# A message-passing layer in one fused kernel: source rows spread by transfers, row tiles every nine chunks, six more picks

## The chip, the cores and the metric

The kernel runs on one core of one Trainium2 chip. The time is device time in microseconds, from start to end of one execution, and lower is better. A core has five engines that run their own instruction streams and meet at semaphores: TensorE (PE, with its weight loads PEld), VectorE (DVE), ScalarE (ACT), GpSimd (POOL) and SyncE (SP). Transfers are sent from the queues of SyncE and ScalarE, and, where they gather rows by an index, from GpSimd.

## What is computed

One layer of a graph network over 6250 nodes and 200000 edges, with 64 features on each, then a residual sum and a layer norm. The edges are sorted by `dst`; `src` is random.

```python
features = H[id_Xe[0]]                                   # H = x, id_Xe = (src, dst)
M_in = jnp.concatenate([features, Xe], axis=1)           # Xe = edge_attr
Y = jax.nn.relu(M_in @ M_W.T + M_b)
Z = jax.ops.segment_sum(Y, id_Xe[1], num_segments=H.shape[0])
H_next = jax.nn.relu(jnp.concatenate([H, Z], axis=1) @ U_W.T + U_b)
out = _layernorm(x + H_next)
```

## The kernel before

The product of the message matrix with the node part is made once for each node, not for each edge: `Y = x @ Wn.T + M_b`, kept in SBUF and stored to DRAM as `Y_rows`. Then the edges go by in 195 chunks of 1024 (8 tiles of 128), and a rest of 320 edges, which the code calls chunk 195 (`NC`). For each chunk the row of Y at each edge's source must be added to the product of its edge features. There are three ways to get those rows for a tile:

- **gathered** (line 399): GpSimd sends one indirect transfer for each tile, which reads 128 rows of `Y_rows` by index (of `x` itself in the first 5 chunks).
- **picked** (lines 705, 731, 741, 949): the sources of the tile are spread over all partitions, ScalarE subtracts the partition's own number (`match`, line 522), VectorE compares the result with the start of each of the 49 blocks of nodes (`onehot_src`, one instruction of 128x6272 elements), and TensorE multiplies the result with Y, 49 products in bf16 on three parts of Y side by side. VectorE sums the three parts. Tile 7 of every chunk from 5 on is picked, and tile 6 too in the chunks that `picked_tiles` names: 249 picks.
- **row by row** (line 368, `load_rows` of SyncE): for tile 6 of the chunks in `row_chunks` SyncE loads node numbers into its registers and sends one transfer of 256 B for each row. The 128 rows of a tile are spread over the steps of several chunks before it (`row_steps`). ScalarE copies the tile into its place (`copy_rows`, line 535).

The rest of a chunk c: SyncE loads the edges (lines 331 and 332, three buffers; it waits until the transposes of chunk c-3 are done), TensorE turns them (line 900), ScalarE copies them (line 508), TensorE multiplies them with the edge weights (`add_edges`, line 918), VectorE adds the rows of Y (`add_rows`, line 725), which waits for that chunk's gathers, ScalarE rectifies (line 528), TensorE sums the messages by destination with a one-hot window of 72 nodes (line 956), and VectorE adds the window to `XZ` (line 749).

Each engine's order is written out by hand. TensorE in round c: edges of c, windows of c-1, transposes of c+1, `spread_src(c + 2)` (line 936), picks of c+1. `spread_src` is a product of one column of the identity with the sources, kept as floats in `src_ones`, and puts a row of 128 or 256 sources onto all partitions of `p_bc`. ScalarE in round c: copy of the turned edges of c+1, match of c+2, rectification of c, copy of a row tile of c+1. VectorE in round c: sums of the picks of c, window comparison of c, window of c-1, `add_rows(c)`, then `copy_match` and comparison for c+2. GpSimd gathers up to six chunks ahead (`G = 6`, it waits for `s_rows_added`), and afterwards adds and multiplies by the means and deviations of the layer norm. After the last chunk come the update product (lines 1002 and 1013) and the layer norm in groups of 8 blocks.

Of the kernel before, what the change touches and what calls it, by code (L numbers as in the profile page):

```python
# [6 lines left out]
def gnn_residual_layernorm_kernel(  # L7
# [13 lines left out]
    i32 = mybir.dt.int32  # L21
# [5 lines left out]
    P = 128  # L27
# [37 lines left out]
    def picked_tiles(c):  # L65
        if not X <= c < NC:
            return []
        return [TILES - 2, TILES - 1] if c % 3 == 0 and c % 48 else [TILES - 1]

    ROWS_TILE = TILES - 2
    ROWS_EVERY = 12
    ROWS_AT_ONCE = 12
    row_chunks = [c for c in range(2 * ROWS_EVERY + 1, NC, ROWS_EVERY) if ROWS_TILE not in picked_tiles(c)]
    row_steps = {row_chunks[t] - s: (t, P - s * ROWS_AT_ONCE - ROWS_AT_ONCE)
                 for t in range(len(row_chunks)) for s in range(-(-P // ROWS_AT_ONCE))}
# [32 lines left out]
                edge_values[T1:NE].rearrange("(p j) -> p j", p=TP))  # L110

    edge_tail = (edge_attr[T0:T1, :].rearrange("(p j) d -> p (j d)", p=P), edge_attr[T1:NE, :])
    dst_tail_row = dst[T0:NE].rearrange("(c n) -> c n", c=1)
    x_blocks = x[0:NFULL * W, :].rearrange("(b p) d -> p b d", p=W)
    out_blocks = out[0:NFULL * W, :].rearrange("(b p) d -> p b d", p=W)
# [2 lines left out]
    with ctx:  # L118
        def sb(name, shape, dt=fp32):
            return ctx.enter_context(nc.sbuf_tensor(name, shape, dt))  # L120
# [7 lines left out]
        def sem(name):  # L128
# [14 lines left out]
        messages = [sb(f"messages{u}", [P, TILES * D]) for u in range(SLOTS)]  # L143
        onehot = [sb(f"onehot{u}", [P, TILES, WIN]) for u in range(SLOTS)]
        onehot_src = [sb(f"onehot_src{u}", [P, NW, P], bf16) for u in range(SLOTS)]
        match = [sb(f"match{u}", [P, 2 * P], i16) for u in range(2)]

        XZ = sb("XZ", [P, NW * W + W])
# [21 lines left out]
        u_bias = sb("u_bias", [D, 1])  # L170

        src_rows = [onehot_src[1][:, 8 * h:8 * h + 16, :].rearrange("p b e -> p (b e)").bitcast(i32)
                    for h in (0, 2)]
        dst_rows = [XZ[:, h * CHUNK:(h + 1) * CHUNK].bitcast(i32) for h in range(2)]
        src_float = [onehot_src[0][:, 16 * h:16 * h + 16, :].rearrange("p b e -> p (b e)").bitcast(fp32)
                     for h in range(2)]
        src_ones = [sb(f"src_ones{h}", [P, CHUNK - RUN]) for h in range(2)]
        dst_float = [onehot_src[2][:, 16 * h:16 * h + 16, :].rearrange("p b e -> p (b e)").bitcast(fp32)  # L180
                     for h in range(2)]
        dst_tail = sb("dst_tail", [1, TAIL], i32)
# [48 lines left out]
        s_dst_tail_loaded = sem("s_dst_tail_loaded")  # L231
        s_src_float = sem("s_src_float")
        s_dst_float = sem("s_dst_float")
        s_src_ones = sem("s_src_ones")
        s_index_T = sem("s_index_T")
        s_index_even = sem("s_index_even")
        s_index_odd = sem("s_index_odd")
# [29 lines left out]
        s_chunk_added = sem("s_chunk_added")  # L267
        s_window = sem("s_window")
        s_window_added = sem("s_window_added")
        s_src_spread = sem("s_src_spread")  # L270
        s_match = sem("s_match")
        s_match_copied = sem("s_match_copied")
        s_onehot_src = sem("s_onehot_src")
# [113 lines left out]
        @block.gpsimd  # L387
        def _(pool):
            nc.gpsimd.memset(ident[:, :], 0.0).then_inc(s_ident, 1)
            pool.wait_ge(s_ident, 1)  # L390
            nc.gpsimd.affine_select(out=ident[:, :], in_=ident[:, :], compare_op=ALU.not_equal, fill=1.0,
                                    base=0, pattern=[[-1, P]], channel_multiplier=1).then_inc(s_ident, 1)
            nc.gpsimd.iota(count[:, :], pattern=[[1, WIN]], base=0, channel_multiplier=0)
            nc.gpsimd.iota(window_start_i[:, :], pattern=[[WIN, NWIN]], base=0, channel_multiplier=0)
            nc.gpsimd.iota(block_start_i[:, :], pattern=[[W, NW]], base=0, channel_multiplier=0)
            nc.gpsimd.iota(node_i[:, :], pattern=[[1, 1]], base=0, channel_multiplier=1).then_inc(s_iota, 1)

            def gather(c, j, index, table, parts=P):
                nc.gpsimd.indirect_dma_start(  # L399
                    out=gathered[c % G][0:parts, j * D:(j + 1) * D], out_offset=None, in_=table,  # L400
                    in_offset=bass.IndirectOffsetOnAxis(ap=index, axis=0),
                ).then_inc(s_gathered[c % G], 16)

            pool.wait_ge(s_src_first_loaded, 16)
            for c in range(X):
                for j in gathered_tiles(c):
                    gather(c, j, src_first[:, c, j:j + 1], x[:, :])

            pool.wait_ge(s_Y_stored, 16 * stores)
            pool.wait_ge(s_index_even, 2)  # L410
            pool.wait_ge(s_index_odd, 2)
            for c in range(X, NC):
                if c >= G:

                    pool.wait_ge(s_rows_added, c - G + 1)
                for j in gathered_tiles(c):
                    gather(c, j, src_all[:, c, j:j + 1], Y_rows)
            pool.wait_ge(s_src_last_loaded, 2 * 16)
            pool.wait_ge(s_rows_added, NC - G + 1)
            for j in gathered_tiles(NC):  # L420
                parts = TP if j == TT - 1 else P
                gather(NC, j, src_last[0:parts, j:j + 1], Y_rows, parts)

            def apply_to_rows(g, values, op, done):
                b0, b1 = groups[g]
                nc.gpsimd.tensor_tensor(h[:, b0:b1, :], h[:, b0:b1, :],  # L426
                                        values[:, b0:b1].unsqueeze(2).to_broadcast([P, b1 - b0, D]),
                                        op).then_inc(done, 1)

            for g in range(len(groups) + LAG + 1):  # L430
                if g < len(groups):
                    pool.wait_ge(s_mean, g + 1)
                    apply_to_rows(g, mean, ALU.add, s_centered)
                if g > LAG:
                    pool.wait_ge(s_scale, g - LAG)
                    apply_to_rows(g - LAG - 1, std, ALU.mult, s_normed)

        @block.scalar
        def _(act):
# [10 lines left out]
            act.dma_start(dst_tail[:, :], dst_tail_row).then_inc(s_dst_tail_loaded, 16)  # L450
            act.dma_start(dst_first[:, :, :], first_chunks(dst)).then_inc(s_dst_first_loaded, 16)

            act.wait_ge(s_eps, 1)
            nc.scalar.activation(std[:, 0:1], eps_col[:, 0:1], ACT.Sqrt)

# [19 lines left out]
                rows_to_float(h0, dst_rows, dst_float, s_dst_rows_loaded, s_dst_float)  # L475
            copy_even_index(4, dst_all)
            copy_even_index(6, dst_all)
            for h0, (b0, n) in enumerate(halves):
                nc.scalar.copy(src_ones[h0][0:n, :], src_rows[h0][0:n, RUN:CHUNK]).then_inc(s_src_ones, 1)

            def copy_block_start(b0, b1):
                nc.scalar.copy(block_start[:, b0:b1, :], block_start_i[:, b0:b1].unsqueeze(2)  # L482
                               .to_broadcast([P, b1 - b0, P])).then_inc(s_block_start, 1)
# [31 lines left out]
            def match_src(c):  # L515

                q, n = c - X, len(picks_of[c]) * P
                act.wait_ge(s_src_spread, q + 1)
                if q >= 2:

                    act.wait_ge(s_match_copied, q - 1)
                nc.scalar.activation(match[q % 2][:, 0:n], p_bc[:, 0:n], ACT.Identity,  # L522
                                     bias=minus_node[:, 0:1]).then_inc(s_match, 1)

            def rectify(c):
# [15 lines left out]
            copy_edges_T(0)  # L541
            copy_x_rows_T(0)
            for c in range(NC + 1):
                if c < NC:
                    copy_edges_T(c + 1)
                if c + 1 < X:
                    copy_x_rows_T(c + 1)
                if picks_of[c + 2]:
                    match_src(c + 2)
                rectify(c)  # L550
                if c + 1 in row_chunks:
                    copy_rows(c + 1)
                if c < 2:
                    copy_middle(c)
                    copy_block_start((0, X_FIRST)[c], (X_FIRST, NW)[c])
                elif X < c <= X + 2:
                    two = c - X - 1
                    nc.scalar.copy(x_rows_of[:, :, two, :], pairs_T[two * D:(two + 1) * D, :, :])
                elif c == X + 3:
                    nc.scalar.copy(XZ[0:D, NFULL * W:NW * W],  # L560
                                   x_pairs_T[0:D, NFULL // 2 * W:(NFULL // 2 + 1) * W]).then_inc(s_XZ, 1)
# [260 lines left out]
        def _(pe):  # L822
# [101 lines left out]
                                                w_gathered[:, :], start=False, stop=(q == PAIRS - 1))  # L924
                last.then_inc(s_summed, 1)

            def spread_src(c):

                q, j = c - X, picked_tiles(c)[0]
                h0, n = (0, P) if c < P else (1, NB)  # L930
                if q == 0:
                    pe.wait_ge(s_src_ones, 2)
                if q >= 1:

                    pe.wait_ge(s_match, q)
                nc.tensor.matmul(p_bc[:, 0:(TILES - j) * P],  # L936
                                 ident[0:n, c - h0 * P:c - h0 * P + 1].to_broadcast([n, P]),
                                 src_ones[h0][0:n, j * P - RUN:CHUNK - RUN],
                                 start=True, stop=True).then_inc(s_src_spread, 1)

            def pick(k):
                if k == 0:
                    pe.wait_ge(s_Y_low, 2)
# [27 lines left out]
            def chunks(windows):  # L971
                transpose_edges(0)
                transpose_x_rows(0)
                for c in range(NC + 1):
                    add_edges(c)
                    if c > 0:
                        windows(c - 1)
                    if c < NC:
                        transpose_edges(c + 1)
                    if c + 1 < X:  # L980
                        transpose_x_rows(c + 1)
                    if picks_of[c + 2]:
                        spread_src(c + 2)
                    for k in picks_of[c + 1]:
                        pick(k)
                windows(NC)
# [61 lines left out]
```

## Time and profile before

| | |
|---|---|
| median of three runs | 1671.68 us (1670.69 to 1673.19) |
| the profiled execution | 1672.69 us, its span 1670.8 us |
| TensorE busy | 1630.3 us, 98% |
| VectorE busy | 1327.9 us, 79% |
| GpSimd busy | 1242.5 us, 74% |
| ScalarE busy | 322.4 us, 19% |
| granted TensorE clock, mean | 0.994 of full speed |

The profile is of one execution. An engine's busy time leaves out its gaps and the instructions that only issue a transfer, so 74% does not say yet how much room an engine has: whether an engine waits for another is told by its waits, and by the order of its instructions in time. Lines are those of the kernel file.

### The profile page before, as it was taken

What the parts mean: (1) busy time and instruction counts of PE and PEld (TensorE: products, weight loads), DVE (VectorE), ACT (ScalarE), POOL (GpSimd) and SP (SyncE); (2) the same over time, 40 slices, a digit from 0 to 9 for tenths busy, and PEclk for the clock granted to TensorE, in tenths of its full rate; (3) what the DMA queues carried; (4) which work ended last, traced back from release to release, by engine and by line L of the source; (5) the groups of instructions that cost most, each with busy time, mean ns of one, the idle gap of its engine ahead of it and who ended that gap; (6) DMA issues with size and microseconds to landing.
All of it is one profiled execution on the core that took longest, in us unless ns stands there. A gap on an engine that the chain in (4) does not pass through costs nothing.

```text
span 1670.8 us, 48392 instructions
## 1 busy us (share of the span) xinstructions
PE 1630.3 (98%) x18304; PEld 1564.1 (94%) x18304; DVE 1327.9 (79%) x1364; ACT 322.4 (19%) x662; POOL 1242.5 (74%) x1323
## 2 busy tenths in 40 slices
PE   5899999999999999999999999999999999999995
PEld 5899999999999999999999999999999999999992
DVE  5787887887888888788788788788778878878873
ACT  4431111111111111111111111111111111111113
POOL 6777777777777777777777777777777777777773
PEclk9999999999999999999999999999999999999997
DMA  7222222222222222222222222222222222222221
GB/s 167 64 65 58 56 66 60 55 66 59 60 60 60 60 59 60 60 60 60 66 60 60 60 60 60 59 61 60 60 59 60 65 55 60 63 57 59 66 43 41
DMA packets 147453, 104.09 MB, mean 62 GB/s; under 512 B 100874, under 2 KB 125418, under 8 KB 147216
## 3 DMA queue, kind: packets, MB, share of 16 engines
q0 software_dynamic: 41568, 42.63, 13.2%
q1 hardware_dynamic: 104530, 56.69, 13.2%
q8 instruction: 148, 2.42, 0.6%
q10 hardware_dynamic: 1118, 1.62, 0.4%
q14 instruction: 89, 0.73, 0.2%
HBM read 97.62 MB, written 3.20 MB: 60 GB/s over the span
## 4 chain that ended last, share of the span: by engine, by line
PE 96%; DVE 1%; ACT 1%; issue 0%; DMA 0%; POOL 0%; DVEq 0%; SPq 0%; POOLq 0%; ACTq 0%
PE p_pick L949 60%; PE p_messages L956 13%; PE p_messages L918 11%; PE p_edges_T L900 7%; PE p_bc L936 3%; PE p_messages L1002 1%; DMA u_stage<-in_L_gnn_U_W_dram 0%; ACT block_start L482 0%; DVE XZ L684 0%; POOL Y L426 0%; PE p_messages L857 0%; PE p_edges_T L868 0%; DVE onehot_src L741 0%; PE p_pick L832 0%; ACT Y_parts L493 0%
## 5 line engine op out<-in xcount | busy, mean ns | idle before, releaser
L399 POOL DMA_INDIRECT gathered<-Y_rows,src_all x1256 | 1185.3, 944 | 383.0 <-issue 379.6
L949 PE MATMUL p_pick<-Y_parts,onehot_src 128*128 128x192 bf16 x12201 | 1037.8, 246 | 0.4 <-DVE onehot_src L741 0.4
L949 PEld LDWEIGHTS p_pick<-Y_parts,onehot_src 128*128 128x128 bf16 x12201 | 1012.6, 98 | 10.6 <-issue 0.7
L741 DVE TENSOR_TENSOR onehot_src<-p_dve,block_start 128x6272 bf16<-128x6272 int16 x249 | 847.1, 3421 | 6.5
L508 ACT COPY edges_T<-p_edges_T 128x512 f32<-128x512 f32 x196 | 114.5, 584 | 1174.3 <-PE p_edges_T L900 1174.3
L956 PE MATMUL p_messages<-onehot,messages 128*64 128x72 f32 x3126 | 237.5, 229 | 2.0 <-ACT messages L528 2.0
L956 PEld LDWEIGHTS p_messages<-onehot,messages 128*64 128x64 f32 x3126 | 208.5, 137 | 25.6 <-ACT messages L528 2.5
L918 PE MATMUL p_messages<-w_edges,edges_T 128*128 128x128 f32 x1564 | 213.0, 279 | 4.9 <-ACT edges_T L508 4.8
L918 PEld LDWEIGHTS p_messages<-w_edges,edges_T 128*128 128x128 f32 x1564 | 190.7, 192 | 6.2 <-ACT edges_T L508 3.4
L705 DVE TENSOR_REDUCE gathered<-p_pick 128x64 f32<-128x192 f32 x249 | 86.9, 349 | 92.6 <-PE p_pick L949 92.6
L696 DVE SCALAR_TENSOR_TENSOR onehot<-p_dve,base,dst_all 128x576 f32<-128x576 f32 x195 | 157.4, 807 | 0.0
L749 DVE TENSOR_TENSOR XZ<-XZ,p_messages 64x72 f32 x196 | 45.7, 233 | 135.6 <-PE p_messages L956 133.6
L528 ACT ACTIVATE messages<-p_messages 128x512 f32<-128x512 f32 x196 | 117.0, 597 | 130.9 <-DVE p_messages L725 128.0
L725 DVE TENSOR_TENSOR p_messages<-p_messages,gathered 128x512 f32<-128x512 f32 x191 | 133.3, 698 | 6.5 <-issue 0.6
L900 PE MATMUL p_edges_T<-ident,edges 128*128 128x128 f32 x782 | 128.4, 287 | 2.9 <-issue 2.9
L900 PEld LDWEIGHTS p_edges_T<-ident,edges 128*128 128x128 f32 x782 | 82.1, 141 | 18.1 <-issue 3.0
L731 DVE TENSOR_SCALAR p_dve<-match 128x64 int32<-128x64 int32 x190 | 46.6, 245 | 57.8 <-ACT match L522 57.8
L936 PE MATMUL p_bc<-src_ones,ident 128*128 128x128 f32 (+1 forms) x380 | 85.9, 308 | 0.0
L522 ACT ACTIVATE match<-p_bc,minus_node 128x128 int16<-128x128 f32 x190 | 77.1, 406 | 0.0
L936 PEld LDWEIGHTS p_bc<-src_ones,ident 128*128 128x128 f32 (+1 forms) x380 | 57.4, 191 | 0.0
L399 POOL DMA_INDIRECT gathered<-in_x_dram,src_first x40 | 40.5, 1012 | 15.3 <-issue 11.9
L426 POOL TENSOR_TENSOR Y<-Y,mean 128x512 f32<-128x512 f32 (+1 forms) x7 | 6.5, 934 | 21.7 <-DVE mean L800 21.7
(101 smaller groups left out, 203.0 us busy)
## 6 DMA issues: line engine op xcount, KB each, us to landing
edges<-in_edge_attr_dram SPq DMA_DIRECT2D x190, 192.0 KB
row_tile<-Y_rows SPq DMA_DIRECT2D x1920, 0.2 KB
gathered<-Y_rows,src_all POOLq DMA_INDIRECT x1256
edges<-in_edge_attr_dram SPq DMA_DIRECT2D x191, 64.0 KB
Y_rows<-Y SPq DMA_DIRECT2D x6, 256.0 KB
out_dram<-Y SPq DMA_DIRECT2D x6, 256.0 KB
edges<-in_edge_attr_dram SPq DMA_DIRECT2D x5, 256.0 KB
xb<-in_x_dram SPq DMA_DIRECT2D x1, 768.0 KB
```

Source lines behind the costliest of these rows:

```text
L399: nc.gpsimd.indirect_dma_start(out=gathered[c % G][0:parts, j * D:(j + 1) * D], out_offset=None, in_=table, in_offset=bass.IndirectOffsetO ...
L508: nc.scalar.copy(edges_T[c % SLOTS][:, 0:pairs * P], p_edges_T[:, 0:pairs * P]).then_inc(s_edges_T_copied, 1)
L528: nc.scalar.activation(messages[c % SLOTS][:, 0:pairs * P], p_messages[c % SLOTS][:, 0:pairs * P], ACT.Relu).then_inc(s_messages, 1)
L696: nc.vector.scalar_tensor_tensor(out=onehot[c % SLOTS][:, 0:tiles, :], in0=count_b[:, 0:tiles, :], scalar=start, in1=nodes.unsqueeze(2).to ...
L705: nc.vector.tensor_reduce(gathered[c % G][:, j * D:(j + 1) * D], p_pick[k % 2][:, 0:3 * D].rearrange("p (t d) -> p d t", d=D), AX.X, ALU.a ...
L725: nc.vector.tensor_tensor(sums, sums, gathered[c % G][:, 0:cols], ALU.add).then_inc(s_rows_added, 1)
L741: nc.vector.tensor_tensor(onehot_src[k % SLOTS][:, :, :], sources.unsqueeze(1).to_broadcast([P, NW, P]), block_start[:, :, :], ALU.is_equa ...
L900: last = nc.tensor.transpose(p_edges_T[:, q * P:(q + 1) * P], edges[u][:, q * P:(q + 1) * P], ident[:, :])
L918: last = nc.tensor.matmul(p_messages[u][:, q * P:(q + 1) * P], edges_T[u][:, q * P:(q + 1) * P], w_edges[:, :], start=(q == 0), stop=(c >= ...
L936: nc.tensor.matmul(p_bc[:, 0:(TILES - j) * P], ident[0:n, c - h0 * P:c - h0 * P + 1].to_broadcast([n, P]), src_ones[h0][0:n, j * P - RUN:C ...
L949: last = nc.tensor.matmul(p_pick[k % 2][:, 0:3 * D], onehot_src[k % SLOTS][:, b, :], Y_parts[:, b, :], start=(b == 0), stop=(b == NW - 1))
L956: last = nc.tensor.matmul(p_windows[u], messages[u][:, j * D:(j + 1) * D], onehot[u][:, j, :], start=(j == 0), stop=(j == tiles - 1))
```

## The change

- `picked_tiles`: tile 6 is picked in every chunk whose number divides by 3, and in those with c % 72 == 4 (76 and 148). 255 picks instead of 249.
- A row tile in every ninth chunk instead of every twelfth, 20 instead of 15, with 16 rows in each step instead of 12.
- The spread of the sources leaves TensorE. ScalarE issues, four chunks ahead, a transfer that reads 128 or 256 sources of the chunk from DRAM and writes them to all 128 partitions of `src_spread` (three buffers, a semaphore for each). The match reads that buffer. In ScalarE's order the match and this transfer stand ahead of the copy of the turned edges. Three of the transfers are issued at the very start.
- GpSimd has a drain between its last gather and the update.

```diff
-        return [TILES - 2, TILES - 1] if c % 3 == 0 and c % 48 else [TILES - 1]
+        return [TILES - 2, TILES - 1] if c % 3 == 0 or c % 72 == 4 else [TILES - 1]
-    ROWS_EVERY = 12
-    ROWS_AT_ONCE = 12
+    ROWS_EVERY = 9
+    ROWS_AT_ONCE = 16
...
+        src_spread = [sb(f"src_spread{u}", [P, 2 * P], i32) for u in range(SLOTS)]
...
+            pool.drain()
+
             def apply_to_rows(g, values, op, done):
...
+            def spread_src(c):
+
+                q, j = c - X, picked_tiles(c)[0]
+                if q >= SLOTS:
+
+                    act.wait_ge(s_match, q - SLOTS + 1)
+                act.dma_start(src_spread[q % SLOTS][:, 0:(TILES - j) * P],
+                              src_chunks[c][:, j * P:CHUNK].to_broadcast([P, (TILES - j) * P])
+                              ).then_inc(s_src_spread[q % SLOTS], 16)
+
+            for c in range(X, X + SLOTS):
+                spread_src(c)
...
-            for h0, (b0, n) in enumerate(halves):
-                nc.scalar.copy(src_ones[h0][0:n, :], src_rows[h0][0:n, RUN:CHUNK]).then_inc(s_src_ones, 1)
...
-                act.wait_ge(s_src_spread, q + 1)
+                act.wait_ge(s_src_spread[q % SLOTS], 16 * (q // SLOTS + 1))
...
-                nc.scalar.activation(match[q % 2][:, 0:n], p_bc[:, 0:n], ACT.Identity,
+                nc.scalar.activation(match[q % 2][:, 0:n], src_spread[q % SLOTS][:, 0:n], ACT.Identity,
...
             for c in range(NC + 1):
+                if picks_of[c + 2]:
+                    match_src(c + 2)
+                if X + SLOTS <= c + 4 < NC:
+                    spread_src(c + 4)
                 if c < NC:
                     copy_edges_T(c + 1)
                 if c + 1 < X:
                     copy_x_rows_T(c + 1)
-                if picks_of[c + 2]:
-                    match_src(c + 2)
...
-            def spread_src(c):
...
-                nc.tensor.matmul(p_bc[:, 0:(TILES - j) * P],
-                                 ident[0:n, c - h0 * P:c - h0 * P + 1].to_broadcast([n, P]),
-                                 src_ones[h0][0:n, j * P - RUN:CHUNK - RUN],
-                                 start=True, stop=True).then_inc(s_src_spread, 1)
...
-                    if picks_of[c + 2]:
-                        spread_src(c + 2)
```

## Rows read from the trace of the kernel before

**Rows 1.** The page: the chain that ended last, shares of the span by line

```profile
PE p_pick L949 60%; PE p_messages L956 13%; PE p_messages L918 11%; PE p_edges_T L900 7%; PE p_bc L936 3%; PE p_messages L1002 1%; DMA u_stage<-in_L_gnn_U_W_dram 0%; ACT block_start L482 0%; DVE XZ L684 0%; POOL Y L426 0%; PE p_messages L857 0%; PE p_edges_T L868 0%; DVE onehot_src L741 0%; PE p_pick L832 0%; ACT Y_parts L493 0%
```

**Rows 2.** The chain in order of time: start us, us, what

```profile
107.84 0.22 PE p_bc L936 x2
108.07 4.04 PE p_pick L949 x49
...
114.76 0.43 PE p_bc L936 x2
```

**Rows 3.** GpSimd's waits (us, times, longest); line 399's duration ns min/median/max, first and last start

```profile
POOL gathered L399 <- issue: 392.5, 1287, 0.3
POOL Y L426 <- DVE mean L800: 21.7, 6, 15.4
POOL gathered L399 <- DVE p_messages L725: 3.0, 10, 0.3
...
L399 POOL DMA_INDIRECT gathered<-Y_rows,src_all x1256: 940/944/961, 58.0 to 1625.1; - x180
```

**Rows 4.** Timeline at the loop's end: start us, us, engine, line, op [idle before]

```profile
1625.07 0.94 POOL L399 DMA_INDIRECT gathered<-Y_rows,src_all  x1 [0.30 <-issue]
...
1628.81 0.91 POOL L399 DMA_INDIRECT gathered<-Y_rows,src_last  x1 [0.30 <-issue]
...
1629.54 0.70 DVE L725 TENSOR_TENSOR p_messages<-p_messages,gathered 128x512 f32<-128x512 f32 x1
...
1632.56 0.37 DVE L725 TENSOR_TENSOR p_messages<-p_messages,gathered 128x192 f32<-128x192 f32 x1
```

**Rows 5.** Stretch of 200 us: busy PE, PEld, DVE, ACT, POOL, clock, DMA share

```profile
200.00:400.00 200.00, 200.00 (x2291) 193.92 (x2289) 162.96 (x160) 34.17 (x75) 151.07 (x161) 1.00 0.27 60
```

**Rows 6.** Timeline: the last gather from x and who reads it

```profile
56.80 0.94 POOL L399 DMA_INDIRECT gathered<-in_x_dram,src_first  x1 [0.30 <-issue]
...
59.55 0.60 PE L907 MATMUL p_pick<-ident,gathered 128*128 128x128 f32 x4
```

**Rows 7.** Timeline of SyncE's queue

```profile
135.28 4.81 SPq L368 DMA_DIRECT2D row_tile<-Y_rows  x12
...
703.70 0.37 SPq L331 DMA_DIRECT2D edges<-in_edge_attr_dram  x1
704.11 1.36 SPq L332 DMA_DIRECT2D edges<-in_edge_attr_dram  x1
706.64 4.85 SPq L368 DMA_DIRECT2D row_tile<-Y_rows  x12
711.54 0.36 SPq L331 DMA_DIRECT2D edges<-in_edge_attr_dram  x1
...
718.12 0.44 SPq L332 DMA_DIRECT2D edges<-in_edge_attr_dram  x1
719.49 3.20 SPq L368 DMA_DIRECT2D row_tile<-Y_rows  x8
...
1597.84 4.84 SPq L368 DMA_DIRECT2D row_tile<-Y_rows  x12
```

**Rows 8.** SyncE's waits: us in total, times, longest

```profile
SPq L331 <- PE p_edges_T L900: 400.0, 97, 10.1
```

**Rows 9.** Timeline of ScalarE in the loop

```profile
729.93 0.26 ACT L535 COPY gathered<-row_tile 128x64 f32<-128x64 f32 x1
...
817.55 0.58 ACT L508 COPY edges_T<-p_edges_T 128x512 f32<-128x512 f32 x1 [5.58 <-PE p_edges_T L900]
```

**Rows 10.** Timeline of the first issues, and the landing of the bias broadcast

```profile
0.76 0.45 SPq L310 DMA_DIRECT2D src_first<-in_src_dram  x1
...
0.76 1.06 ACTq L443 DMA_DIRECT2D onehot_src<-in_src_dram  x2
...
14.98 0.77 SPq L319 DMA_DIRECT2D m_bias<-in_L_gnn_M_b_dram  x1
...
m_bias<-in_L_gnn_M_b_dram SPq DMA_DIRECT2D x1, 32.0 KB, 4.0
```

More of the change, by code:

```diff
@@ L112, in gnn_residual_layernorm_kernel @@
     edge_tail = (edge_attr[T0:T1, :].rearrange("(p j) d -> p (j d)", p=P), edge_attr[T1:NE, :])
+    src_chunks = src[0:NC * CHUNK].rearrange("(c a n) -> c a n", a=1, n=CHUNK)
     dst_tail_row = dst[T0:NE].rearrange("(c n) -> c n", c=1)
@@ L178, in gnn_residual_layernorm_kernel @@
                      for h in range(2)]
-        src_ones = [sb(f"src_ones{h}", [P, CHUNK - RUN]) for h in range(2)]
         dst_float = [onehot_src[2][:, 16 * h:16 * h + 16, :].rearrange("p b e -> p (b e)").bitcast(fp32)
@@ L233, in gnn_residual_layernorm_kernel @@
         s_dst_float = sem("s_dst_float")
-        s_src_ones = sem("s_src_ones")
         s_index_T = sem("s_index_T")
@@ L269, in gnn_residual_layernorm_kernel @@
         s_window_added = sem("s_window_added")
-        s_src_spread = sem("s_src_spread")
+        s_src_spread = [sem(f"s_src_spread{u}") for u in range(SLOTS)]
         s_match = sem("s_match")
@@ L925, in add_edges @@
                 last.then_inc(s_summed, 1)
-            def spread_src(c):
[L929 to L935, printed above, removed]
-                nc.tensor.matmul(p_bc[:, 0:(TILES - j) * P],
-                                 ident[0:n, c - h0 * P:c - h0 * P + 1].to_broadcast([n, P]),
-                                 src_ones[h0][0:n, j * P - RUN:CHUNK - RUN],
-                                 start=True, stop=True).then_inc(s_src_spread, 1)
             def pick(k):
```

## Prediction

> **What bounds the kernel now.** I read the page first: the chain that ended last runs over TensorE's lines, 60 + 13 + 11 + 7 + 3% of the span, and the 3% is the line this change deletes [rows 1]. That suggests TensorE alone sets the pace. The chain in order of time gives the prices of its pieces: a pick is 4.04 us; from its end (112.11 us) to the next spread at 114.76 us a chunk takes 2.65 us for its products, windows and transposes; the spread itself is 0.22 us for one tile of sources and 0.43 us for two [rows 2].
>
> Then I asked who waits on the other engines, since a second engine may stand just behind. GpSimd spends nearly nothing on waiting: 3.0 us for VectorE, and 392.5 us of "issue", which is 1287 gaps of 0.3 us, one before each gather [rows 3]. So it issues its gathers back to back from 5.4 to 1629.7 us, 1299 of them (40 + 1256 + 3) with hardly a pause. The last four start from 1625.07 to 1628.81, three periods of 1.247 us [rows 4]. The durations run from 940 to 961 ns over all 1256 [rows 3], so the period is a fixed price. The last gather ends at 1629.7 us and VectorE adds the last rows at 1632.56 us [rows 4]: GpSimd arrives only 2.8 us before it is needed. The kernel has two bounds that finish together.
>
> SyncE is the third. In its queue a step of one chunk is two edge loads, a stretch that loads the node numbers into registers, and twelve row transfers; the step from 703.70 to 711.49 us leaves 0.05 us before the next edge load starts at 711.54 [rows 7]. Its total spare time is 400.0 us of waiting for TensorE's transposes [rows 8].
>
> **Part 1, the spread leaves TensorE.** 190 spreads go, 131 of one tile and 59 of two: 131 x 0.22 + 59 x 0.43 = 54.2 us off TensorE's path [rows 2]. Six picks come (249 to 255: chunks 48, 96, 144 and 192 by the first clause, 76 and 148 by the second), 6 x 4.04 = 24.2 us. TensorE's own sum is 30.0 us shorter.
>
> **Part 2, GpSimd.** Five more row tiles (15 to 20) and six more picks take 11 gathers away: 11 x 1.247 = 13.7 us, so its last gather ends at 1629.7 - 13.7 = 1616.0 us. This is the smaller of the two savings, so GpSimd becomes the bound and some 16 us of TensorE's gain turn into waits of VectorE's addition for gathers. Per nine chunks GpSimd issues 3 x (7 + 7 + 6) - 1 = 59 gathers, 73.6 us, while TensorE needs 9 x 2.65 + 12 x 4.04 = 72.3 us [rows 2]. VectorE is busy 163 of 200 us in the loop [rows 5]; it has room to catch up behind a late gather, so such a delay isn't cumulative.
>
> Behind the last gather comes its landing time L. The trace has no landing for gathers. The nearest row: the last gather from x (L399, gathered<-in_x_dram) ends at 57.74 us and TensorE reads its tile at 59.55 us, straight after its previous work [rows 6], so L is at most 1.8 us there, and at least 0. I take 1.8. From the last addition at 1632.56 us to the end of the span 38.2 us pass and stay as they are. New span: 1616.0 + 1.8 + 38.2 = 1656.0 us. The addition of chunk 194 can't be in the way: it needs 3.0 us to the next addition (1629.54 to 1632.56), and the three last gathers take 3.7 us.
>
> What a page says of L: the Trainium skill, "DMA: Bandwidth & Descriptors", section "Anatomy of one DMA — SWDGE (gpsimd) path", gives such a transfer a fixed cost of about 2.0 us from issue to completion. The trace agrees as far as it goes (at most 0.94 + 1.8 us from start to use). Counted so, as an estimate, the last rows would be there at 1615.1 + 2.0 us and the span 0.7 us shorter.
>
> **Part 3, SyncE.** Rows go from 1920 to 2560, in steps of 16. Over the 143 full steps of twelve, from 135.28 to 1597.84 us [rows 7], the edge loads, register loads and rows take 7.02 us in the mean (I averaged the timeline; single ones run 6.8 to 7.4). Four rows more cost (4.93 - 3.23) = 1.70 us by the difference between the mean twelve and the mean of the 15 first steps of eight, or 4 x 0.41 by the mean per row; the register stretch ahead of the rows grows from 0.93 us (eight rows, 718.56 to 719.49) to 1.17 (twelve, 705.47 to 706.64), so another 0.2 for four [rows 7]. A step of 16 is 8.9 us, with the gap behind it 8.94. Eight steps and a chunk without rows (0.98 us) are 72.5 us per nine chunks, against GpSimd's 73.6. It is hidden with only 1.1 us to spare in each tile. Within a tile the steps run behind the transposes by up to 8 x 8.9 - 55 - 8.9 = 7 us (55 us is what TensorE needs for seven chunks, two of them with two picks: 7 x 2.65 + 9 x 4.04). The rows of one tile end at 711.49 us, 7.8 us after the trigger of their step (703.70), and ScalarE copies them at 729.93 us, 26 us after it [rows 7, 9]. Now 7 + 8.9 = 16 us plus a landing are set against those 26: still in time. The edge loads have three chunks (some 24 us) of lead: hidden.
>
> **Part 4, ScalarE.** Each chunk gains one transfer issue. No row shows one in the loop; bounds from the start: 0.53 us for a plain load on this queue, 0.77 us for a broadcast to 128 partitions on SyncE's [rows 10]. I take 0.6. After its rectification ScalarE sits idle 5.58 us until the next transposes [rows 9]; the match and the issue fit there, as the transfer was sent two chunks ahead (the bias broadcast took 4.0 us to land [rows 10], two chunks are 16 us). Behind the match wait the copy of the transposed edges and the rectification; both are released later anyway. If that cover were gone, 190 x 0.6 us would be 114 us, but ScalarE is busy 34 of 200 us [rows 5]. At the start three issues stand ahead of ScalarE's first conversion: TensorE begins 1.6 to 2.3 us later. GpSimd's first 40 gathers don't depend on it, so it costs nothing now. VectorE loses its 57.8 us of waits for the match, which was no bound.
>
> **Part 5, the drain.** It stands after the last gather, where GpSimd waits 15.4 us for the first mean [rows 3]: between 0 and that, taken as 0.
>
> **Sum.** Span 1656.0 us. The span of before is 1670.8, its execution 1672.69, the median of the three runs 1671.68: 0.9 above the span. Forecast 1656.9 us.
>
> **Rivals.**
> *A, GpSimd bound, as above:* 1655.1 (L = 0) to 1659 us (L = 4), 0.62.
>
> *B, SyncE becomes the bound.* Mechanism: the row tile's last step comes too late, ScalarE waits at the copy of the rows, and copies of transposed edges queue behind that. For: 1.1 us of spare per tile, some second edge loads of 1.36 us instead of 0.44 [rows 7], and a queue of ScalarE that now sends a row to each of 128 partitions in every chunk beside it. Against: the first issues of both queues ran side by side at 0.45 and 0.53 us each, less than the later 0.77 alone [rows 10], and the DMA engines are busy 27% [rows 5]. The Trainium skill says in the same page, section "Issuing engines are not separate DMA queues", that transfers started by any engine end up on the same 16 DMA engines and interleave; it gives no price for that. Price: the first step starts near 97 us; twenty periods P = 8s + 1, the five chunks behind the last row tile (38 us) and the tail (38) give a span of 172 + 20P. It passes 1656 at s = 9.15 us and 1671 at s = 9.24. With 0.5 us of contention in each step (s = 9.45) the span is 1704. Slower by over 0.2%: 0.17; between, 1660 to 1672: 0.05.
>
> *C, small stalls:* VectorE's comparison starts only after a late addition, two-pick chunks then start picking late, and the end finds TensorE behind: 3 to 10 us. For: the three engines are within 2% of each other; against: GpSimd never waits for them, having six buffers. 1659 to 1667 us, 0.11.
>
> *D, TensorE was the only bound:* 1671.7 - 30.0 + 1 = 1643 us, would need gathers faster than the 940 ns minimum: 0.02.
>
> *E, nothing moves:* something keeps the end where it is, 1670 to 1673: 0.03.
>
> **Chances and range.** What a measurement of this kernel tells from no change is 0.2%, 3.3 us. Faster: A, C, D and most of the middle of B, 0.78; same 0.05; slower 0.17. The range reaches from A's lower bound over C and B's middle: 1654.5 to 1669 us.
>
> **What would show it.** GpSimd: 1248 gathers in the loop and after it, period 1.247 us, the last ending near 1616 us. VectorE's addition (line 725) with some 15 us of new idle before it, and TensorE with as much. SyncE's steps near 8.9 us with 20 to 90 us of waiting for transposes left. ScalarE's copy of rows with no wait before it. I am wrong if SyncE's steps pass 9.15 us, if gathers take longer than 944 ns, or if GpSimd waits for buffers.

## The result, and the profile after

The changed kernel takes 1654.38 us in the median of four runs (1653.16 to 1655.23), the kernel before beside it 1672.09 us. The ratio is 0.9894, with a 95% interval of 0.9880 to 0.9908. Faster was forecast, and it is; but the time was forecast as 1656.9 us with a range from 1654.5 to 1669 us, and lies 2.5 us below the forecast and just under the range.

The page of the changed kernel: span and busy times, then the chain that ended last by engine and line, and three groups (line, engine, operation, count; busy, mean ns of one; idle time before and what ended it).

```profile
span 1651.4 us, 50341 instructions
PE 1602.5 (97%) x18218; PEld 1542.1 (93%) x18218; DVE 1337.4 (81%) x1376; ACT 338.0 (20%) x665; POOL 1231.4 (75%) x1312
...
POOL 69%; issue 23%; PE 5%; DVE 1%; ACT 1%; ACTq 0%; DMA 0%; POOLq 0%; DVEq 0%
POOL gathered L398 69%; PE p_pick L949 2%; PE p_messages L1000 1%; PE p_messages L956 1%; PE p_messages L932 0%; DVE XZ L698 0%; POOL Y L428 0%; PE p_edges_T L914 0%; PE p_edges_T L882 0%; PE p_messages L871 0%; PE p_messages L937 0%; PE p_pick L846 0%; DVE most L646 0%; ACT block_start L494 0%; DVE least L645 0%
...
L398 POOL DMA_INDIRECT gathered<-Y_rows,src_all x1245 | 1175.2, 944 | 379.6 <-issue 379.3
...
L739 DVE TENSOR_TENSOR p_messages<-p_messages,gathered 128x512 f32<-128x512 f32 x191 | 133.3, 698 | 93.0 <-DMA gathered<-Y_rows,src_all 73.7
```

TensorE is still busy 97%, and yet the chain has changed its engine. Before, it ran over TensorE's lines from start to end [rows 1]; now 69% of the span is the gathers themselves and 23% the gaps before them. The mean gather is as long as before, 944 ns [rows 3]. New is that VectorE's addition waits 73.7 us for gathers, 50 times; before, it had no such wait. Busy shares would have told none of this.

The waits of the changed kernel (engine line <- who ended the wait: us in total, times, longest).

```profile
ACT messages L540 <- DVE p_messages L739: 296.5, 121, 5.9
DVE p_messages L739 <- DMA gathered<-Y_rows,src_all: 73.7, 50, 4.5
...
PE p_messages L956 <- ACT messages L540: 7.7, 4, 4.6
...
PE p_pick L949 <- DVE onehot_src L755: 5.8, 9, 1.3
...
SPq L330 <- PE p_edges_T L914: 66.0, 21, 9.9
```

VectorE's 73.7 us of waiting are mostly absorbed by queued work: TensorE itself waits 13.5 us in these two lines. SyncE's waiting for transposes has gone from 400.0 us [rows 8] to 66.0.

The end of the loop in the timeline of the changed kernel (start us, us, engine, line).

```profile
1612.76 0.70 DVE L739 TENSOR_TENSOR p_messages<-p_messages,gathered 128x512 f32<-128x512 f32 x1 [4.46 <-DMA gathered<-Y_rows,src_all]
...
1614.04 0.90 POOL L398 DMA_INDIRECT gathered<-Y_rows,src_last  x1 [0.30 <-issue]
1614.14 2.18 PE L956 MATMUL p_messages<-onehot,messages 128*64 128x72 f32 x16 [4.62 <-ACT messages L540]
1616.47 0.23 DVE L763 TENSOR_TENSOR XZ<-XZ,p_messages 64x72 f32 x1 [2.54 <-PE p_messages L956]
1616.73 0.37 DVE L739 TENSOR_TENSOR p_messages<-p_messages,gathered 128x192 f32<-128x192 f32 x1
```

The last gather ends at 1614.94 us, against 1629.72 before [rows 4], and the last addition starts 1.79 us behind it.

**Where 19.4 us of span went** (1670.8 to 1651.4): the last gather ends 14.8 us earlier (13.7 were forecast), the stretch from it to the last addition is 1.05 us shorter (2.84 to 1.79), and the stretch from there to the end is 3.6 us shorter (38.2 to 34.7), where none was forecast. The two profiled executions lie apart by more than the medians, 19.5 us against 17.7: the one of before was 0.6 us slower than the median of the four runs of that kernel, the one of the changed kernel was the fastest of its four, 1.2 us below their median.

Most of what made the last part shorter stands in the instructions of line 118 (before) and 119 (after), the end of the program. First the kernel before, then the changed one (duration ns min/median/max, first and last start us), each with GpSimd's last multiplication (start us, us) from the timeline.

```profile
L118 POOLq DRAIN  x1: 8518/8518/8518, 1662.0 to 1662.0; - x1
L118 SPq COMPARE_BRANCH  x1: 38/38/38, 1667.8 to 1667.8; - x1
L118 SPq DRAIN  x1: 7/7/7, 1668.0 to 1668.0; - x1
...
1660.87 3.29 POOL L426 TENSOR_TENSOR Y<-Y,std 128x512 f32<-128x512 f32 x4
```

```profile
L119 POOLq DRAIN  x1: 2206/2206/2206, 1645.2 to 1645.2; - x1
...
L119 SPq DRAIN  x1: 7/7/7, 1651.1 to 1651.1; - x1
...
1644.00 3.29 POOL L428 TENSOR_TENSOR Y<-Y,std 128x512 f32<-128x512 f32 x4
```

Before, SyncE had seen its last store land and reached its own drain at 1668.0 us, but GpSimd's closing drain ran until 1670.5. After, GpSimd's is over at 1647.4 and SyncE is the last. That is 2.5 us, as much as the miss. The experiments below test it. A closing drain's record starts while GpSimd's last multiplications still run: before, it ends 6.4 us behind them, after, 0.1 us. So of the 8.5 us some 2 are ordinary work, and so are the 2.2 us of the changed kernel.

### The profile page after: what moved, and what is told of

Its sections match the earlier page's. It is cut to its first block, busy times and chain, and to the rows that moved or that the text cites. A ratio compares the mean times of both kernels' runs of the same rounds, so it can differ in the third digit from the quotient of the medians.

```text
span 1651.4 us, 50341 instructions
## 1 busy us (share of the span) xinstructions
PE 1602.5 (97%) x18218; PEld 1542.1 (93%) x18218; DVE 1337.4 (81%) x1376; ACT 338.0 (20%) x665; POOL 1231.4 (75%) x1312
## 4 chain that ended last, share of the span: by engine, by line
POOL 69%; issue 23%; PE 5%; DVE 1%; ACT 1%; ACTq 0%; DMA 0%; POOLq 0%; DVEq 0%
POOL gathered L398 69%; PE p_pick L949 2%; PE p_messages L1000 1%; PE p_messages L956 1%; PE p_messages L932 0%; DVE XZ L698 0%; POOL Y L428 0%; PE p_edges_T L914 0%; PE p_edges_T L882 0%; PE p_messages L871 0%; PE p_messages L937 0%; PE p_pick L846 0%; DVE most L646 0%; ACT block_start L494 0%; DVE least L645 0%
## 5 line engine op out<-in xcount | busy, mean ns | idle before, releaser
L949 PE MATMUL p_pick<-Y_parts,onehot_src 128*128 128x192 bf16 x12495 | 1061.9, 246 | 6.8 <-DVE onehot_src L755 5.8
L949 PEld LDWEIGHTS p_pick<-Y_parts,onehot_src 128*128 128x128 bf16 x12495 | 1035.7, 98 | 11.5 <-issue 8.2
L755 DVE TENSOR_TENSOR onehot_src<-p_dve,block_start 128x6272 bf16<-128x6272 int16 x255 | 867.0, 3421 | 6.5
L739 DVE TENSOR_TENSOR p_messages<-p_messages,gathered 128x512 f32<-128x512 f32 x191 | 133.3, 698 | 93.0 <-DMA gathered<-Y_rows,src_all 73.7
L534 ACT ACTIVATE match<-src_spread,minus_node 128x128 int16<-128x128 int32 x190 | 81.8, 431 | 0.0
L1000 PE MATMUL p_messages<-XZ,w_update 128*64 128x512 f32 (+1 forms) x26 | 14.8, 662 | 2.5 <-issue 2.5
L846 PE MATMUL p_pick<-ident,onehot_src 128*128 128x128 f32 (+1 forms) x32 | 7.0, 386 | 6.6 <-DVE dst_all L640 3.6
```

The source lines that it names most:

```text
L534: nc.scalar.activation(match[q % 2][:, 0:n], src_spread[q % SLOTS][:, 0:n], ACT.Identity, bias=minus_node[:, 0:1]).then_inc(s_match, 1)
L739: nc.vector.tensor_tensor(sums, sums, gathered[c % G][:, 0:cols], ALU.add).then_inc(s_rows_added, 1)
L755: nc.vector.tensor_tensor(onehot_src[k % SLOTS][:, :, :], sources.unsqueeze(1).to_broadcast([P, NW, P]), block_start[:, :, :], ALU.is_equa ...
L949: last = nc.tensor.matmul(p_pick[k % 2][:, 0:3 * D], onehot_src[k % SLOTS][:, b, :], Y_parts[:, b, :], start=(b == 0), stop=(b == NW - 1))
```

## The experiments

My theory: the end of the kernel is the latest of three queues that hardly wait for each other, GpSimd's gathers, TensorE's products and SyncE's row steps; the change takes TensorE from the first to the second place. The rivals: TensorE alone; SyncE already; and, for the missing 2.5 us, chance in the profile or the drain.

**One part alone: the spread.** `picked_tiles`, `ROWS_EVERY` and `ROWS_AT_ONCE` are those of before, all else is the changed kernel.

```diff
-        return [TILES - 2, TILES - 1] if c % 3 == 0 or c % 72 == 4 else [TILES - 1]
+        return [TILES - 2, TILES - 1] if c % 3 == 0 and c % 48 else [TILES - 1]
-    ROWS_EVERY = 9
-    ROWS_AT_ONCE = 16
+    ROWS_EVERY = 12
+    ROWS_AT_ONCE = 12
```

> The spread of the sources is sent by ScalarE as in the change; picks (249), row tiles (15) and rows per step (12) are those of before, and so are the 1256 gathers. My theory, GpSimd's chain of gathers sets the end: TensorE has 54 us less to do and the time hardly moves. GpSimd's last gather should end at 1628.6 us (the start of the Y gathers 1.3 us earlier, as after the change), and 1.8 us plus the tail of 34.7 to 38.2 us behind it give a span of 1665 to 1668.6 us. Rival, TensorE alone is the bound: 54 us less, a span near 1617 us. Also: if the issues on ScalarE are what brought the Y gathers forward, they start at 56.7 us here; if not, at 58.0.

Measured: 1667.79 us (1666.73 to 1670.63), a ratio of 0.9974 (0.9962 to 0.9985), span 1668.7 us. TensorE has 54 us less to do and the kernel gains 4.3 us, of which the drain, which this kernel also has and which alone gives 2.8 us (below), can explain a good half. The Y gathers start at 57.1 us, between the two values that I had set against each other, so that side question stays open here. The last gather ends at 1631.7 us, 3 us later than forecast, since a gather takes 947 ns in the median in this execution instead of 944; this execution is the slowest of seven, 2.8 us above their median. The waits say where the 54 us went.

```profile
ACT messages L540 <- DVE p_messages L739: 480.2, 158, 5.9
...
DVE p_messages L739 <- DMA gathered<-Y_rows,src_all: 157.4, 87, 5.2
...
PE p_pick L949 <- DVE onehot_src L755: 36.6, 43, 1.3
```

TensorE now stands still before 43 picks, because the comparisons for them start behind additions that wait for gathers. TensorE as the only bound falls.

**The other part alone: the counts.** The kernel before with the three settings of the change, the spread still on TensorE.

```diff
-        return [TILES - 2, TILES - 1] if c % 3 == 0 and c % 48 else [TILES - 1]
+        return [TILES - 2, TILES - 1] if c % 3 == 0 or c % 72 == 4 else [TILES - 1]
-    ROWS_EVERY = 12
-    ROWS_AT_ONCE = 12
+    ROWS_EVERY = 9
+    ROWS_AT_ONCE = 16
```

> 255 picks, 20 row tiles and 16 rows per step, with the spread left on TensorE as before. TensorE's sum grows by 6 picks (24.2 us) and six wider spreads (1.3 us) while GpSimd saves 11 gathers (13.7 us). My theory, the later of the two ends counts: TensorE, span 1670.8 + 25.5 = 1696 us. Rival, gathers alone decide: 1657 us. SyncE, at 9.0 us for each step, has room again since the chunks are longer.

Measured: 1699.69 us (1698.63 to 1700.2), ratio 1.016 (1.0143 to 1.0177), span 1698.3 us. The chain is TensorE's again (96%) and GpSimd waits for means instead of the other way round:

```profile
PE 96%; DVE 1%; ACT 1%; issue 0%; DMA 0%; POOL 0%; DVEq 0%; SPq 0%; POOLq 0%; ACTq 0%
...
POOL Y L426 <- DVE mean L800: 55.1, 6, 48.8
...
SPq L118 <- PEq L118: 4.7, 1, 4.7
```

The forecast of 1696 is short by 2.3 us; in this run SyncE waits 4.7 us at the end of the program for GpSimd's closing drain, which took 10478 ns, where the kernel before waits 2.7 us. So the two halves are worth -4 us (with the drain) and +28 us alone, and -18 us together. They don't add up: each moves a different queue, and only the later one counts.

**How far GpSimd's bound reaches: 8 and 24 gathers less.** The changed kernel without the gather of tile 0 in every 24th, or every 8th, chunk. It leaves out rows that the result needs and keeps the other instructions, so it shows a time and computes other messages. Shown for every 24th chunk, which is 8 gathers less:

```diff
-                if j not in picked_tiles(c) and not (c in row_chunks and j == ROWS_TILE)]
+                if j not in picked_tiles(c) and not (c in row_chunks and j == ROWS_TILE) and not (j == 0 and c % 24 == 2 and c > 2)]
```

> The kernel after the change with 8 gathers left out (tile 0 of every 24th chunk keeps what its buffer held, so those messages use other rows). My theory: GpSimd ends 8 x 1.248 = 10.0 us earlier and the span follows it, 1651.4 - 10.0 = 1641.4 us, since TensorE's own end lies near 1638 to 1641 us of span (1670.8 - 30.0, and up to 3 us of shorter tail). Rival, SyncE or TensorE already sets the pace after the change: the span stays within 3 us of 1651.

> The kernel after the change with 24 gathers left out (tile 0 of every 8th chunk keeps what its buffer held). GpSimd alone would end 30 us earlier, at a span of 1621 us. My theory: TensorE takes over, so the span stops at its floor of 1638 to 1641 us. If SyncE's row steps are the next bound (20 periods of 73.0 us from 97 us on, and 75 us behind them) that alone would be 1631 us, below TensorE's. Rival, no other bound within 30 us: 1621 us.

Measured: 1643.65 us (span 1641.7) without 8, and 1639.93 us (span 1638.8) without 24; ratios to before 0.9828 (0.9812 to 0.9845) and 0.9802 (0.9786 to 0.9819). The first 8 gathers give 9.7 us of span, 1.2 us each, a gather's full period. The next 16 give 2.9 us instead of 20. (The medians say 10.7 and 3.7 us.) The chains of the two kernels, 8 gathers less first:

```profile
PE 46%; POOL 37%; issue 13%; DVE 2%; ACT 1%; ACTq 0%; DMA 0%; POOLq 0%; DVEq 0%
```

```profile
PE 96%; DVE 1%; ACT 1%; issue 0%; ACTq 0%; POOL 0%; DVEq 0%; POOLq 0%
...
POOL Y L428 <- DVE mean L814: 36.3, 6, 30.0
```

TensorE's floor is a span of 1638.8 us, 12.6 below the changed kernel. GpSimd is the bound there, and TensorE is next.

**SyncE's turn: one more transfer in each row step.** The changed kernel, with a 17th row per step, into a tile that nobody reads.

```diff
+        row_extra = sb("row_extra", [P, D])
...
+        s_extra = sem("s_extra")
...
+                sp.dma_start(row_extra[r0 // ROWS_AT_ONCE:r0 // ROWS_AT_ONCE + 1, :], Y_rows[0:1, :]).then_inc(s_extra, 16)
                 for r, end in zip(range(r0, r1), ends):
...
+            sp.wait_ge(s_extra, 16 * len(row_steps))
```

> The kernel after the change, and in each of the 160 row steps SyncE sends one more row, into a tile that nobody reads. A step grows from 8.96 to 9.37 us. Theory of the third bound: nine chunks then need 8 x 9.42 + 0.98 = 76.3 us of SyncE, more than GpSimd's 73.6; the last row lands near 97 + 20 x 76.3 = 1623 us instead of 1571, and with the 72 us behind it the span is 1693 to 1698 us, while GpSimd begins to wait for free buffers. Rival, SyncE still has its 66 us of waits to spend: 160 x 0.41 = 66 us are absorbed, and the span stays at 1651 to 1655 us.

Measured: 1669.17 us (1663.92 to 1670.29), ratio 0.9978 (0.9965 to 0.9992), span of the profiled execution 1662.1 us. Neither number came true as written. The mechanism came true in part: SyncE has 21% of the chain, and the copy of rows and the transposes now wait for its transfers. But GpSimd does not begin to wait for buffers, as I had expected: its gathers run on undisturbed (5 waits of at most 0.3 us for VectorE, the last gather starts at 1614.4 us).

```profile
PE 38%; POOL 23%; SPq 21%; issue 14%; DVE 2%; DMA 2%; ACT 1%; ACTq 0%; DVEq 0%; POOLq 0%
...
ACT gathered L551 <- DMA row_tile<-Y_rows: 31.6, 11, 4.4
...
PE p_edges_T L918 <- DMA edges<-in_edge_attr_dram: 15.5, 12, 3.2
```

The size was off because I priced the extra row at 0.41 us. That is a row whose address comes from a register. This one has a fixed address:

```profile
815.32 0.27 SPq L368 DMA_DIRECT2D row_extra<-Y_rows  x1
815.78 6.41 SPq L370 DMA_DIRECT2D row_tile<-Y_rows  x16
822.24 0.36 SPq L332 DMA_DIRECT2D edges<-in_edge_attr_dram  x1
```

From edge load to edge load the step takes 9.19 us in the mean of 155 steps, against 9.02 in the changed kernel (156 steps). The prediction's formula, 172 + 20 x (8 x 9.19 + 0.98), gives a span of 1662.0 us, and 1662.1 was measured in the profiled execution. That it fits to the tenth is luck: this is the fastest of five executions, and three of the others have spans of 1667.4 to 1668.5 us. So 0.17 us more in a step of 9.02 moves the end from GpSimd to SyncE and costs over 10 us of span, 14.8 us in the median.

**The drain, taken away.** One line less in the changed kernel.

```diff
-            pool.drain()
```

> The changed kernel without GpSimd's drain. It stands where GpSimd waits 13 us for the first mean, so I expect no difference: within 1 us of the changed kernel, 1653.5 to 1655.5 us. If the drain cost its wait for transfers at the end, or shortened the tail, this would differ by 1 us or more.

Measured: 1659.77 us (1659.07 to 1660.16), ratio 0.9926 (0.991 to 0.9943), against 0.9894 (0.9880 to 0.9908) with it: 5.4 us slower. I had expected no difference, and that was wrong. The end of the program in this kernel:

```profile
L119 POOLq DRAIN  x1: 10483/10483/10483, 1647.6 to 1647.6; - x1
L119 SPq COMPARE_BRANCH  x1: 38/38/38, 1653.4 to 1653.4; - x1
...
SPq L119 <- PEq L119: 4.7, 1, 4.7
```

The closing drain takes 10.5 us instead of 2.2 and ends 4.5 us after everything else. The remaining 0.9 us of the medians lies within their intervals. The two profiled executions lie 7.0 us apart: besides the 4.5, the gathers start 1.1 us later here (57.8 against 56.7 us, long before any drain) and end 1.3 us later, and the first mean comes 1.1 us later behind the last addition.

**The drain, added alone.** The kernel before with nothing but that line.

```diff
+
+            pool.drain()
```

> The kernel before with nothing but GpSimd's drain behind its last gather. In the kernel before the drain at the end of the program takes 8518 ns, and ends at 1670.5 us, 2.5 us after SyncE is done at 1668.0; with the earlier drain that closing one took 2206 ns in four runs. My theory: the early drain does this work under GpSimd's wait for the first mean, the closing drain shrinks to 2.2 us, and the time falls by 2.5 us, to a ratio of 0.9985. Rival, the early drain only moves the same work or costs its own: no change or slower by up to 1 us.

Measured: 1669.56 us (1668.35 to 1671.38, 11 runs), ratio 0.9986 (0.9977 to 0.9995), the expected one. In its trace the closing drain is short. The early one's record starts while gathers still run, and reaches to 1635.4 us: 6.4 us behind the end of the last gather (1629.0) and well ahead of the first mean (1643.0), for which GpSimd waits anyway:

```profile
L424 POOLq DRAIN  x1: 21282/21282/21282, 1614.1 to 1614.1; - x1
```

```profile
L118 POOLq DRAIN  x1: 2207/2207/2207, 1660.0 to 1660.0; - x1
```

Both directions agree, so the drain's gain is shown; its size is less sharp, as the interval of this run alone reaches from 0.8 to 3.8 us. The changed kernel has the same pattern:

```profile
L424 POOLq DRAIN  x1: 23247/23247/23247, 1600.0 to 1600.0; - x1
```

It ends at 1623.25 us, 8.3 us behind the last gather. All twelve traces fit one account: the first drain behind the gathers has a remainder of several us beyond GpSimd's own last instruction, wherever it stands. In the three kernels with 249 picks and 15 row tiles it is 6.4 us (one closing, two early drains), in the nine others 7.7 to 8.3 us (two closing, seven early). So the closing drain of 8.5 us belongs to the one set of counts and those of 10.5 us to the other, and how the sources are spread makes no difference to it. What a drain does in that time, and why the counts change it, is open; I did not try it.

**Versions beyond the change.** Two more picks (40 and 112), one more row tile (chunk 10, steps from chunk 3), and both. An assertion on the number of row tiles changes with the second edit and is not shown.

```diff
-        return [TILES - 2, TILES - 1] if c % 3 == 0 or c % 72 == 4 else [TILES - 1]
+        return [TILES - 2, TILES - 1] if c % 3 == 0 or c % 36 == 4 and c < 180 else [TILES - 1]
...
-    row_chunks = [c for c in range(2 * ROWS_EVERY + 1, NC, ROWS_EVERY) if ROWS_TILE not in picked_tiles(c)]
+    row_chunks = [c for c in range(ROWS_EVERY + 1, NC, ROWS_EVERY) if ROWS_TILE not in picked_tiles(c)]
```

> Tile 6 is also picked in chunks 40 and 112: 257 picks, two gathers fewer than after the change. GpSimd bound: 2.5 us earlier, a time near 1652 us. TensorE gets 8.1 us more: its floor of 1638.8 us of span rises to 1646.9, still below 1648.9, so my theory expects 2 to 2.5 us of gain over the changed kernel. Rival, TensorE already shares the bound through stalls behind late gathers: no gain or a loss up to 5 us.

> The changed kernel with one more row tile, for chunk 10, so that the row steps begin at chunk 3: 21 row tiles, one gather fewer. GpSimd bound: 1.25 us less, about 1653.1 us. Against it stands that SyncE's steps of 9 us then lie in the first chunks, which TensorE does in 5 us each, and hold back the edge loads; my theory says that TensorE has some 12 us to lose before that shows, so the gain stays. Rival: the early loads come too late and the time grows by up to 10 us.

> The changed kernel with chunks 40 and 112 picked too and the extra early row tile: 257 picks, 21 row tiles, 3 gathers fewer. GpSimd bound: 3 x 1.25 = 3.7 us below the changed kernel's 1654.4, about 1651 us; TensorE's floor is at 1647 us of span, so it can just follow. Rival: the row steps in the first chunks and the two picks together take TensorE's remaining room, and the time is that of two more picks alone (1652.2) or more.

Measured: 1652.18 us (0.9882, 0.9865 to 0.9898), 1653.93 us (0.9892, 0.9875 to 0.9908) and 1652.02 us (0.9881, 0.9865 to 0.9896). All beat the kernel before. Against the changed kernel's 0.9894 (0.9880 to 0.9908) the intervals overlap, so these gains of 0.5 to 2.4 us are of the expected sign but are not shown. The third is not better than the first although it has one gather less, as its rival said. Its chain and SyncE's wait:

```profile
PE 80%; POOL 7%; SPq 5%; issue 4%; DVE 1%; ACT 1%; DMA 0%; ACTq 0%; POOLq 0%; DVEq 0%
...
SPq L330 <- PE p_edges_T L914: 8.5, 11, 5.2
```

TensorE has most of the chain again and SyncE has 8.5 us of waiting left: all three queues are nearly full, so I expect little more from moving tiles between the three ways. Other splits were not tried.

## Why the prediction was wrong in its size

- **What bounds the kernel** was right: two queues that end together [rows 3, 4] and a third close behind [rows 7, 8]. The two halves alone, the missing gathers and the 17th row in each step show it.
- **Part 1, TensorE 30.0 us shorter**: right. Its floor, found by leaving out 24 gathers, is a span of 1638.8 us, 32.0 below before, of which 2.5 is the drain: 29.5 us.
- **Part 2, GpSimd 13.7 us shorter, the period fixed at 1.247 us**: right; 14.8 us were measured in the profiled execution. The 1.1 us more can't be put down to the change. The first gathers from x set the start of the others, which lies between 56.7 and 58.6 us in the twelve traces, with and without each part (58.0 before, 56.7 after, 58.1 with the early row tile). Of the 1.3 us between before and after, 0.3 is the start of the first gather, and 0.6 is one gather that ran 2430 ns before and 1834 after, beside VectorE's second step of splitting Y. The timelines of the kernel before and of the changed one:

```profile
47.04 1.76 DVE L671 TENSOR_TENSOR Y_parts<-onehot_src,Y_parts 128x1536 bf16<-128x1536 f32 x1 [2.02 <-ACT Y_parts L493]
...
47.19 2.43 POOL L399 DMA_INDIRECT gathered<-in_x_dram,src_first  x1 [0.30 <-issue]
```

```profile
46.97 1.76 DVE L685 TENSOR_TENSOR Y_parts<-onehot_src,Y_parts 128x1536 bf16<-128x1536 f32 x1 [2.02 <-ACT Y_parts L505]
...
47.71 1.83 POOL L398 DMA_INDIRECT gathered<-in_x_dram,src_first  x1 [0.30 <-issue]
```

  In both, the gather ends 0.8 us after VectorE's instruction, so it is the longer the earlier in that instruction it starts. In the loop VectorE's comparison of 3.42 us, one of whose inputs lies in PSUM, leaves all 1245 gathers of the changed kernel at 940 to 961 ns. The Trainium skill, "SBUF — State Buffer", section "Who interferes with whom", says that a VectorE instruction with two inputs in SBUF contends with a GpSimd instruction that reads SBUF, over a port pair which only one of them holds at a time. The same section also says that a probe saw no such stall of transfers beside `tensor_tensor`, which is VectorE's operation here. The traces agree with the first sentence; no run here tests it alone.
- **The landing, L = 1.8 us**: the last addition starts 1.79 us after the last gather, and this agreement is luck. For the chunk before, where VectorE does wait for the gather, the gather ends at 1611.24 and the addition starts at 1612.76: 1.5 us, or 2.5 us from the gather's start. The last addition waits 0.3 us longer, for VectorE's window, which waits for a slow product. The prediction had said that the addition of chunk 194 can't be in the way, as the next follows 3.0 us behind it; here it follows 3.97 us behind.
- **The 38.2 us behind the last addition, "stay as they are", and Part 5, the drain, "taken as 0"**: this is the step that failed. I allowed the drain a cost between 0 and 15.4 us and no gain, though the program ends with a drain of GpSimd in any case, and the trace of before shows it with 8518 ns, ending 2.5 us after SyncE. The stretch measured 34.7 us. The drain alone is worth 2.8 us of median time (1672.32 to 1669.56), and a forecast with the 2.5 us in it, 1656.9 - 2.5 = 1654.4 us, lies at the measured time. The other 1.1 us of the shorter stretch stand between the last addition and the first mean: 12.3 us before and 11.3 after, 10.9 to 12.9 in the twelve traces, with no order that the changes would explain.
- **The fit to the tenth** is partly luck. Against the forecast span of 1656.0 us the profiled execution, 1651.4, is short by 4.6 us: 1.1 of the gathers' start, 2.5 of the drain and 1.1 of the stretch before the first mean, in rounded numbers. The median time lies 3.0 us above this execution's span, where the prediction added 0.9, and that takes 2.1 us back.
- **The range** begins at 1654.5 us, called rival A's lower bound, which is 1655.1 in the prediction's own sum. Neither holds 1654.38.
- **VectorE's new idle time, "some 15 us"**: 73.7 us for gathers alone. TensorE's, "as much", came out near that: 13.5 us in the two lines above. The waits of VectorE are the longer because it often arrives early and TensorE still has work queued.
- **Part 3, SyncE**: right in kind; 8.94 us per step were forecast and 9.02 measured, 8 x 9.02 + 0.98 = 73.1 us in nine chunks against GpSimd's 73.6. It is hidden with 0.5 us to spare, not 1.1. Rival B was nearer than its 0.22 looked.
- **Part 4, ScalarE**: right. An issue takes 0.33 us in the loop (0.6 were taken). It is sent from the queue while ScalarE rectifies, after an idle stretch of 5.89 us, and no wait for it shows:

```profile
611.09 0.60 ACT L540 ACTIVATE messages<-p_messages 128x512 f32<-128x512 f32 x1 [5.89 <-DVE p_messages L739]
611.18 0.33 ACTq L461 DMA_DIRECT2D src_spread<-in_src_dram  x1
611.58 0.39 ACT L534 ACTIVATE match<-src_spread,minus_node 128x128 int16<-128x128 int32 x1
```

- **Rival C, stalls that leave TensorE behind**: the stalls are there, 9 before picks, 5.8 us in sum, but TensorE's 12.6 us of room take them.

## What to carry to other kernels

When a change takes work from the bound engine, write down for every other queue when its own last instruction would be done, gaps included: the new end is the latest of these, so here 13.7 us of TensorE's 30 were left. An engine with 74% of busy time can be the bound, if its gaps belong to its instructions. And read the drains and barriers at the end of the program as rows with a price: an instruction that "does nothing" may do early, under a wait, what would be paid at the end.

## What I had not expected of the hardware

The first drain of GpSimd behind some 1300 indirect transfers takes 6.4 to 8.3 us beyond the engine's own work, even with 32 us (before) between the last transfer and the drain; a second drain behind it takes 0.1 us beyond it. Its record alone misleads, since it starts while earlier instructions still run: 23.2 us for the early drain of the changed kernel, of which 14.9 lie beside gathers.

A new wait goes with a lower clock. In the changed kernel TensorE idles 4.6 us before its last full window, and the granted clock is at its lower level (1.2 of 2.4 GHz) for most of the next 10 us. The first row is of the kernel before, the others of the changed one; the columns are stretch, length, busy PE, PEld, DVE, ACT, POOL, clock, DMA share, GB/s.

```profile
1630.00:1635.00 5.00, 2.49 (x26) 2.03 (x26) 1.52 (x5) 0.98 (x2) 0.00 (x0) 1.00 0.03 7
```

```profile
1600.00:1610.00 10.00, 8.96 (x100) 8.27 (x99) 2.88 (x6) 1.55 (x3) 7.56 (x8) 1.00 0.14 28
1610.00:1615.00 5.00, 0.86 (x7) 0.86 (x8) 1.14 (x2) 0.60 (x1) 3.73 (x4) 0.59 0.14 26
1615.00:1620.00 5.00, 2.30 (x17) 1.87 (x16) 0.83 (x3) 0.38 (x1) 0.00 (x0) 0.50 0.04 8
1620.00:1625.00 5.00, 3.92 (x8) 1.07 (x8) 0.00 (x0) 0.92 (x2) 0.00 (x0) 0.54 0.02 5
```

The 16 products of the last full window take 2.18 us there, against 1.22 in the loop. Before, the stretch from 1630 to 1635 us still had 1.00, and the drop came only behind it. The spread alone, where TensorE waits 5.3 us at this place, also has 0.50 behind it (1630 to 1635 us); picks and row tile together, where VectorE waits at most 0.5 us for the last gathers, has 1.00 (1610 to 1615 us). The short stalls inside the loop, up to 1.3 us before a pick, leave the clock at 1.00. In the whole it cost little here: from the last addition to the first mean the changed kernel takes 11.3 us, and the kernel before, whose clock fell later, 12.3.
